# Writing out the hardware loops of the head stage and the expert stage

## The chip, the cores and the metric

The kernel runs on one core of a Trainium2 chip. The metric is the device time of one execution in microseconds (us), the median of three runs: 1520.96 us, from 1519.29 to 1521.52. The engines are PE (TensorE, matmuls; PEld is its weight load), DVE (VectorE), ACT (ScalarE), POOL (GpSimd) and SP (SyncE, which issues the DMAs). Each runs an instruction stream of its own; they meet in semaphores only.

## What is computed

One transformer block on x of 4 x 1024 x 128 in float32: a differential attention with 8 heads, then a feed-forward part in which each token's projections are weighted by 16 experts. Cut to what matters:

```python
x = x + attn(layernorm(x))          # B=4, T=1024, 8 heads, D=32, two sub-heads each
#   w = softmax(q1 k1) - lam * softmax(q2 k2);  y = w @ v;  y = gamma * y / rms(y);  y @ Wout
x = x + ffn(layernorm(x))
#   rw = gating(x)                                 # 16 experts
#   q, k, v = sum_e rw[e] * (x @ proj[e])          # head size 64
#   attn = softmax(causal(q k)) @ v                # within a batch
#   out = sum_e rw[e] * attn @ o_proj[e]
```

## The kernel before, in words

**Head stage.** A step is one pair of heads of one batch; there are 16 steps (`STEPS`) of 16 units (`UNITS`). A unit is 128 queries of one head, with its two sub-heads. The engines handle 32 units (`SLOTS`, two steps) in one piece of code, called a pass below, and there are eight passes (`ITERS`). Each engine has its own function for a pass: `slots(it, first, last)` on PE, ACT and DVE, `two_steps` on SP. Pass 0 is written out with `first` and pass 7 with `last`; passes 1 to 6 are one hardware loop, `Fori(1, ITERS - 1)`. POOL goes by half steps of 8 units: `units(h, tail)` stands in two loops, for h 0 to 1 and h 2 to 31.

For each unit PE makes the scores of a sub-head (`scores`, L584) in its half of `score_ps`, DVE takes the row maxima (L1207), ACT the exponentials with their sums (L900). DVE makes the factor of the second sub-head (L1218, L1220), POOL scales and adds (`mix`, L478 and L480), and three units later PE transposes the mixed rows (L607), ACT and DVE copy them to `probT` (L829, L322), and PE multiplies with v (L613). Beside it, at fixed places of a pass, `misc_fill` has PE make the projections of later steps (L562, L567), which ACT and DVE split into two float16 parts (L863, L1126) and SP restacks by DMA (L362). The rms of a finished half step is taken on POOL (`rms`, L485 to L491), and DVE scales by it (L1259).

**Expert stage.** A batch is eight token tiles; `tiles2(it, first, last)` on PE, ACT and DVE handles a batch. Batches 0 and 3 are written out, batches 1 and 2 are `Fori(1, B - 1)`. POOL scales tiles by the expert weights in pairs (L532) in `Fori(1, B * NT // 2)`; SP's part was written out already. DVE's L1412 runs once in each tile.

**What sets the order.** Each engine's order is that of its code; pools or a scheduler have no part in it. All buffers are reused under hand-written semaphore counts. In a loop such a count is an expression of the loop's variable, so it stands in a register and is computed before the wait:

```python
def mix(n, u):
    pool.wait_ge(c_ok, n + 1)
```

Here `n` is `8 * h + u`. Tile addresses that move with the loop go by registers too, such as `resid[:, bass.ds(tile0, 4), :]`.

Of the kernel before, what the change touches and what calls it, by code (L numbers as in the profile page):

```python
# [48 lines left out]
B, T, C = 4, 1024, 128  # L49
NT = T // P  # L50
# [3 lines left out]
STEPS = B * G  # L54
UNITS = 16
ITERS = STEPS // 2
# [86 lines left out]
def block_kernel(nc, x, wq, wkv, wout, lq1, lk1, lq2, lk2, gamma, sim, gates, eq, ek, ev, eo, out):  # L143
    ctx = ExitStack()
    with ctx:
# [183 lines left out]
        def _(sp):  # L329
# [53 lines left out]
            def two_steps(it, first, last):  # L383
                for k in range(2):
                    j = 2 * it + k

                    if not last:
                        token0, column0 = (j + 2) // G * T, (j + 2) % G * P
                        sp.wait_ge(filled["v1"], j + 1)
                        load_step(k, token0, column0)  # L390

                    if not (last and k == 1):
                        stack("k", (k + 1) % 2, j + 1, None if first and k == 0 else UNITS * j)

                    if not last:
                        stack("q", k, j + 2, UNITS * (j + 1))

            two_steps(0, True, False)
            sp.wait_ge(ln_late, 6)
            with sp.Fori(1, ITERS - 1) as it:  # L400
                two_steps(it, False, False)
            two_steps(ITERS - 1, False, True)

# [30 lines left out]
        def _(pool):  # L434
# [58 lines left out]
            def units(h, tail):  # L493

                for u in range(8):
                    mix(8 * h + u, u % 4)
                    if tail and u == RMS_AFTER:
                        rms(h - 2)

            with pool.Fori(0, 2) as h:  # L500
                units(h, False)
            with pool.Fori(2, 2 * STEPS) as h:
                units(h, True)

            pool.wait_ge(g_mean, 1)
# [22 lines left out]
            def scale_by_experts(m, r, peeled):  # L528

                if not peeled:  # L530
                    pool.wait_ge(xs_lo, m)
                pool.tensor_tensor(xs[:, r, :, :], x2n[:, bass.ds(m, 1), :].to_broadcast([P, E, C]),  # L532
                                   rw_all[:, bass.ds(m, 1), :].rearrange("p a e -> p e a").to_broadcast([P, E, C]),
                                   ALU.mult).then_inc(xs_ok, 1)

            scale_by_experts(0, 0, True)
            scale_by_experts(1, 1, False)
            with pool.Fori(1, B * NT // 2) as pair:
                scale_by_experts(2 * pair, 0, False)
                scale_by_experts(2 * pair + 1, 1, False)  # L540

# [2 lines left out]
        def _(pe):  # L544
# [124 lines left out]
                            mm.then_inc(out_ok, 1)  # L669

            slots(0, True, False)
            with pe.Fori(1, ITERS - 1) as it:
                slots(it, False, False)
            slots(ITERS - 1, False, True)

# [142 lines left out]
                    experts(3)  # L818

            tiles2(0, True, False)  # L820
            with pe.Fori(1, B - 1) as it:
                tiles2(it, False, False)
            tiles2(B - 1, False, True)

# [2 lines left out]
        def _(act):  # L827
# [111 lines left out]
                        rsqrt_seed(gs[:, 4, 0:BT], gs[:, 3, 0:BT], gs[:, 2, 0:BT], g_v, 1, g_y, 0)  # L939

            slots(0, True, False)
            with act.Fori(1, ITERS - 1) as it:
                slots(it, False, False)
            slots(ITERS - 1, False, True)

# [90 lines left out]
                                       ACT.Copy, scale=1.0 / WSCALE).then_inc(kv_read, 1)  # L1036

            tiles2(0, True, False)
            with act.Fori(1, B - 1) as it:
                tiles2(it, False, False)  # L1040
            tiles2(B - 1, False, True)

# [2 lines left out]
        def _(dve):  # L1045
# [217 lines left out]
                        ln2_early(s - LN2_SLOT)  # L1263

            slots(0, True, False)
            with dve.Fori(1, ITERS - 1) as it:
                slots(it, False, False)
            slots(ITERS - 1, False, True)

# [145 lines left out]
                                                 op0=ALU.mult, op1=ALU.subtract).then_inc(lo2, 1)  # L1415

            tiles2(0, True, False)
            with dve.Fori(1, B - 1) as it:
                tiles2(it, False, False)
            tiles2(B - 1, False, True)  # L1420

# [21 lines left out]
```

## Time and profile before

| | |
|---|---|
| median of three runs | 1520.96 us |
| profiled execution, its own time | 1519.09 us |
| its span, first to last instruction | 1517.3 us |
| granted TensorE clock, mean | 0.97 |
| instructions in the profile | 26450 |
| code brought by queue q8 | 36 packets, 0.59 MB |
| code brought by queue q14 | 49 packets, 0.40 MB |

The profile is of one execution. Busy time counts the instructions that do work; register, branch, wait and DMA-issuing instructions are not in it. An instruction that is queued begins a little before the one ahead of it ends, so back to back starts overlap by up to a tenth of a microsecond. "issue" as a releaser means that the engine waited for nothing that the profile shows. The granted clock is a share of 2.4 GHz. The head stage spans about 40 to 1130 us, the expert stage about 1190 us to the end; pass 1 begins at 170.

### The profile page before, as it was taken

To read this page: it belongs to the slowest core of one execution; us is meant where nothing else is said; L and a number is where in the kernel's file an instruction comes from. 1 tells how busy PE (TensorE), PEld (TensorE's weight loads), DVE (VectorE), ACT (ScalarE), POOL (GpSimd) and SP (SyncE) were. 2 spreads that over 40 slices of the span, in tenths; PEclk is the share of its full clock that TensorE was granted. 3 is DMA by queue.
4 is the path that set the end of the run, shared out by engine and by line. 5 is a ranking of instruction groups with operands and counts; after the bars stand their busy time and mean duration, and the time that the engine had idled before them with its cause. 6 is when DMAs were issued, how large, how long until landed. Compare 5 with 4: busy or idle time off the path is not lost. (4 is left out here: it accounts for less than half of the span.)

```text
span 1517.3 us, 26450 instructions
## 1 busy us (share of the span) xinstructions
PE 1259.6 (83%) x8370; PEld 745.9 (49%) x8370; DVE 1266.5 (83%) x2033; ACT 1038.6 (68%) x1871; POOL 1107.2 (73%) x715
## 2 busy tenths in 40 slices
PE   3788888888888888888888888888874179999997
PEld 1444444444444444444444444444433179889887
DVE  5898999989998999999999899999986557766664
ACT  2887777777777777777777777777754155555553
POOL 3898888888888888888888888888882443434320
PEclk9899999999999999999999999999996589999999
DMA  4231111111211111111211111111003377777670
GB/s 111 71 81 48 47 29 48 29 47 39 58 34 47 35 39 47 28 48 39 55 35 47 32 43 47 28 30 27 0 1 56 68 129 119 133 117 135 115 125 10
DMA packets 184565, 86.32 MB, mean 57 GB/s; under 512 B 150176, under 2 KB 166048, under 8 KB 184480
## 3 DMA queue, kind: packets, MB, share of 16 engines
q1 hardware_dynamic: 184480, 85.33, 26.4%
q8 instruction: 36, 0.59, 0.2%
q14 instruction: 49, 0.40, 0.1%
HBM read 7.68 MB, written 2.10 MB: 6 GB/s over the span
## 5 line engine op out<-in xcount | busy, mean ns | idle before, releaser
L1207 DVE TENSOR_REDUCE negmax<-score_ps 128x1 f32<-128x1024 f32 x512 | 618.7, 1216 | 87.1 <-PE score_ps L584 85.3
L900 ACT ACTIVATE prob<-score_ps,negmax 128x1024 f32<-128x1024 f32 x512 | 571.6, 1116 | 128.8 <-DVE negmax L1207 116.7
L480 POOL TENSOR_TENSOR prob<-prob 128x1024 f32<-128x1024 f32 x256 | 604.2, 2360 | 21.3
L584 PE MATMUL score_ps<-ka,qa 128*128 128x512 f16 x1024 | 312.4, 387 | 119.5 <-ACT prob L900 106.0
L478 POOL TENSOR_SCALAR prob<-prob,ccol 128x1024 f32<-128x1024 f32 x256 | 287.3, 1122 | 103.9 <-DVE ccol L1220 103.5
L607 PE MATMUL trans_ps<-ident,prob 128*128 128x128 f32 x2048 | 283.3, 276 | 7.4 <-POOL prob L480 3.0
L613 PE MATMUL attn_ps<-probT,v_sb 128*64 128x512 f32 x1024 | 276.6, 620 | 1.1 <-DVE probT L322 1.1
L607 PEld LDWEIGHTS trans_ps<-ident,prob 128*128 128x128 f32 x2048 | 239.5, 142 | 75.5 <-DVE probT L322 17.7
L532 POOL TENSOR_TENSOR xs<-xnT,rw_all 128x2048 f32 (+1 forms) x32 | 115.5, 3611 | 170.4 <-DVE prob L1352 163.7
L584 PEld LDWEIGHTS score_ps<-ka,qa 128*128 128x128 f16 x1024 | 72.4, 98 | 277.9 <-ACT prob L900 234.0
L322 DVE COPY probT<-trans_ps 128x512 f32<-128x512 f32 x256 | 173.9, 679 | 2.4 <-PE trans_ps L607 2.4
L736 PE MATMUL qkv_ps<-ew_split,xsT 128*128 128x192 f16 x1536 | 145.9, 250 | 31.5 <-DMA xsT<-prob 31.5
L829 ACT ACTIVATE probT<-trans_ps 128x512 f32<-128x512 f32 x256 | 152.4, 595 | 20.0 <-PE trans_ps L607 19.9
L736 PEld LDWEIGHTS qkv_ps<-ew_split,xsT 128*128 128x128 f16 x1536 | 129.9, 99 | 34.9 <-issue 31.6
L1352 DVE TENSOR_TENSOR prob<-xs,prob 128x2048 f16<-128x2048 f32 x32 | 73.4, 2292 | 65.8 <-ACT prob L973 65.8
L613 PEld LDWEIGHTS attn_ps<-probT,v_sb 128*64 128x64 f32 x1024 | 51.2, 135 | 109.4 <-issue 109.3
L900 ACT ACTIVATION_READ_ACCUMULATOR prob<-score_ps,negmax 128x1 f32 x512 | 103.1, 201 | 0.0
L973 ACT ACTIVATE prob<-xs 128x2048 f16<-128x2048 f32 x32 | 61.3, 1916 | 32.4 <-POOL xs L532 32.4
L1220 DVE TENSOR_SCALAR ccol<-recip,sums,lam 128x1 f32<-128x1 f32 x256 | 69.9, 273 | 9.4
L1259 DVE TENSOR_TENSOR attn_n<-attn_both,tl 128x512 f32<-128x512 f32 x32 | 72.2, 2257 | 0.1
L863 ACT ACTIVATE split<-misc_ps 128x512 f16<-128x512 f32 x60 | 35.8, 597 | 52.3 <-PE misc_ps L562 52.3
L1010 ACT ACTIVATE prob<-s_ps,nm 128x128 f32<-128x128 f32 (+7 forms) x32 | 23.7, 742 | 68.9 <-DVE nm L1387 68.9
(193 smaller groups left out, 1355.8 us busy)
## 6 DMA issues: line engine op xcount, KB each, us to landing
qa<-split SPq DMA_DIRECT2D x256, 64.0 KB, 2.0
ka<-split SPq DMA_DIRECT2D x256, 64.0 KB, 2.0
xg<-xnT SPq DMA_DIRECT2D x16, 512.0 KB, 3.0
resid<-in_L_attn_x SPq DMA_DIRECT2D x4, 512.0 KB, 5.6
wg<-in_L_attn_Wkv SPq DMA_DIRECT2D x32, 64.0 KB, 1.9
out<-yo SPq DMA_DIRECT2D x32, 64.0 KB, 2.5
wg<-in_L_attn_Wq SPq DMA_DIRECT2D x16, 64.0 KB, 1.9
xsT<-prob SPq DMA_TRANSPOSE x64, 4.5
```

Of the source, the lines that this page charges most:

```text
L322: copy(probT[:, half % 2, 4 * bank:4 * bank + 4, u // 4, (u % 4) * P:(u % 4 + 1) * P], trans_ps[:, bank, :].rearrange("p (k q) -> p k q", ...
L478: pool.tensor_scalar(prob2[:, u, :], prob2[:, u, :], ccol[:, u:u + 1], 1.0, ALU.mult, ALU.mult).then_inc(scaled_P, 1)
L480: pool.tensor_tensor(prob1[:, u, :], prob1[:, u, :], prob2[:, u, :], ALU.add).then_inc(mix_ok, 1)
L532: pool.tensor_tensor(xs[:, r, :, :], x2n[:, bass.ds(m, 1), :].to_broadcast([P, E, C]), rw_all[:, bass.ds(m, 1), :].rearrange("p a e -> p e ...
L584: mm = pe.matmul(score_ps[:, sub, kh * HALF:(kh + 1) * HALF], qa[:, par, head * 2 + sub, q0:q0 + P], ka[:, par, head * 2 + sub, kh * HALF: ...
L607: mm = pe.transpose(trans_ps[:, kb, t * P:(t + 1) * P], prob1[:, u % 4, k0:k0 + P], ident[:, :])
L613: return pe.matmul(attn_ps[head * DV:(head + 1) * DV, :], v_sb[:, (half // 2) % 2, kt, head * DV:(head + 1) * DV], probT[:, half % 2, kt, ...
L736: mm = pe.matmul(qkv_ps[:, 0:3 * DE], xsT[:, t % X_BUFS, x_part, e, :], ew_split[:, w_part, e, :], start=e == 0 and n == 0, stop=e == E - ...
L829: return act.activation(dst, src, ACT.Copy)
L900: act.activation(prob2[:, s % 4, :] if sub else prob1[:, s % 4, :], score_ps[:, sub, :], ACT.Exp, bias=negmax[:, s % 2, sub:sub + 1], accu ...
L1207: dve.tensor_reduce(negmax[:, s % 2, sub:sub + 1], score_ps[:, sub, :], AX.X, ALU.max, negate=True).then_inc(max_ok, 1)
L1352: dve.tensor_tensor(xs_split[:, r, 1, :, :], xs[:, r, :, :], xs_split[:, r, 0, :, :], ALU.subtract).then_inc(xs_lo, 1)
```

## The change

All hardware loops of the two stages are written out: the loop's body is emitted once for each value, `it`, `h` and `pair` are Python integers, and so every count that is waited for and every address is a constant. Nothing else is changed: the same work in the same order on each engine. The nine places:

```diff
@@ sync: two_steps
-            with sp.Fori(1, ITERS - 1) as it:
+            for it in range(1, ITERS - 1):
                 two_steps(it, False, False)
@@ gpsimd: units
-            with pool.Fori(0, 2) as h:
+            for h in range(2):
                 units(h, False)
-            with pool.Fori(2, 2 * STEPS) as h:
+            for h in range(2, 2 * STEPS):
                 units(h, True)
@@ gpsimd: expert stage
-            with pool.Fori(1, B * NT // 2) as pair:
+            for pair in range(1, B * NT // 2):
                 scale_by_experts(2 * pair, 0, False)
                 scale_by_experts(2 * pair + 1, 1, False)
@@ tensor, scalar and vector, head stage (pe, act, dve)
-            with pe.Fori(1, ITERS - 1) as it:
+            for it in range(1, ITERS - 1):
                 slots(it, False, False)
@@ tensor, scalar and vector, expert stage (pe, act, dve)
-            with pe.Fori(1, B - 1) as it:
+            for it in range(1, B - 1):
                 tiles2(it, False, False)
```

In the order of the program ACT has 744 rows before (waits shown) and 1319 with the change, POOL 112 and 673 rows. The end of ACT's head loop, before (L900 the exponential, L829 the copy to `probT`, L863 the split of a projection, L942 the loop itself):

```order
L895 ISA
L900 ACTIVATE prob,sums<-score_ps,negmax 128x1024 [waits trans_ok,max_ok]
L829 ACTIVATE probT<-trans_ps 128x4x128 [waits trans_ok]
L895 REGISTER_ALU
L900 ACTIVATE prob,sums<-score_ps,negmax 128x1024 [waits mix_ok,max_ok]
L863 ACTIVATE split<-misc_ps 128x512 [waits filled_q1]
L942 REGISTER_ALU
L942 COMPARE_AND_BRANCH
```

The same place of ACT with the change, between pass 1 and pass 2:

```order
L900 ACTIVATE prob,sums<-score_ps,negmax 128x1024 [waits trans_ok,max_ok]
L829 ACTIVATE probT<-trans_ps 128x4x128 [waits trans_ok]
L900 ACTIVATE prob,sums<-score_ps,negmax 128x1024 [waits mix_ok,max_ok]
L863 ACTIVATE split<-misc_ps 128x512 [waits filled_q1]
L900 ACTIVATE prob,sums<-score_ps,negmax 128x1024 [waits trans_ok,max_ok]
L829 ACTIVATE probT<-trans_ps 128x4x128 [waits trans_ok]
L900 ACTIVATE prob,sums<-score_ps,negmax 128x1024 [waits mix_ok,max_ok]
L933 ACTIVATE attn_nT<-misc_ps 128x512 [waits cols_ok]
```

The register arithmetic and the jump are gone; L863 is followed by the exponential of the next pass.

POOL inside `units`, before (L478 and L480 are `mix`, L485 to L491 `rms`; L476 is the wait of `mix`, L484 to L490 those of `rms`):

```order
L476 REGISTER_ALU
L478 TENSOR_SCALAR prob<-prob,ccol 128x1024 [waits c_ok]
L480 TENSOR_TENSOR prob<-prob 128x1024 [waits scaled_P]
L484 ISA
L485 TENSOR_TENSOR tl<-tl 128x8 [waits stat_ok]
L486 ISA
L487 TENSOR_TENSOR tl<-tl 128x8 [waits rms_v]
L488 REGISTER_ALU
L489 TENSOR_TENSOR tl<-tl,rms_const 128x8 [waits rms_v]
L490 REGISTER_ALU
L491 TENSOR_TENSOR tl<-tl,rms_const 128x8 [waits rms_v]
L476 REGISTER_ALU
```

And with the change:

```order
L478 TENSOR_SCALAR prob<-prob,ccol 128x1024 [waits c_ok]
L480 TENSOR_TENSOR prob<-prob 128x1024 [waits scaled_P]
L485 TENSOR_TENSOR tl<-tl 128x8 [waits stat_ok]
L487 TENSOR_TENSOR tl<-tl 128x8 [waits rms_v]
L489 TENSOR_TENSOR tl<-tl,rms_const 128x8 [waits rms_v]
L491 TENSOR_TENSOR tl<-tl,rms_const 128x8 [waits rms_v]
L478 TENSOR_SCALAR prob<-prob,ccol 128x1024 [waits c_ok]
```

The instructions that do the work stand as before, and what computed the counts between them is gone.

## Rows read from the trace of the kernel before

**Rows 1.** The page, busy us (share of the span) xinstructions of each engine

```profile
PE 1259.6 (83%) x8370; PEld 745.9 (49%) x8370; DVE 1266.5 (83%) x2033; ACT 1038.6 (68%) x1871; POOL 1107.2 (73%) x715
```

**Rows 2.** Windows of L478: stretch, us, POOL busy (x starts), PEclk, DMA share, GB/s

```profile
136.39:170.35 33.96, 8.98 (x8) 1.00 0.14 32
170.35:272.24 101.89, 26.94 (x24) 1.00 0.18 46
272.24:342.45 70.21, 17.95 (x16) 0.98 0.16 41
342.45:410.37 67.92, 17.95 (x16) 1.00 0.16 42
410.37:479.02 68.65, 17.95 (x16) 1.00 0.16 42
...
546.94:615.60 68.66, 17.96 (x16) 1.00 0.16 42
...
683.51:752.45 68.94, 17.96 (x16) 1.00 0.16 41
...
820.37:889.25 68.88, 17.95 (x16) 1.00 0.16 41
889.25:1025.09 135.84, 35.88 (x32) 1.00 0.15 37
```

**Rows 3.** Waits, 170.35 to 1025.09 us: engine, line, releaser: us, times, longest

```profile
ACT prob L900 <- DVE negmax L1207: 83.4, 145, 2.0
POOL prob L478 <- DVE ccol L1220: 82.1, 105, 1.8
PE score_ps L584 <- ACT prob L900: 79.7, 130, 2.9
DVE negmax L1207 <- PE score_ps L584: 63.9, 127, 1.3
...
ACT prob L900 <- issue: 10.9, 5, 2.4
```

**Rows 4.** Timeline of ACT, second jump: start, us, instruction, [idle before]

```profile
437.43 0.60 ACT L863 ACTIVATE split<-misc_ps 128x512 f16<-128x512 f32 x1 [0.59 <-PE misc_ps L562]
440.10 1.11 ACT L900 ACTIVATE prob<-score_ps,negmax 128x1024 f32<-128x1024 f32 x1 [2.07 <-issue]
```

**Rows 5.** Timeline of DVE at the same jump

```profile
437.50 2.40 DVE L1259 TENSOR_TENSOR attn_n<-attn_both,tl 128x512 f32<-128x512 f32 x1
439.83 0.15 DVE L1218 RECIPROCAL recip<-sums 128x1 f32<-128x1 f32 x1
```

**Rows 6.** DMA queues (packets, MB, share), 170 to 305.8 us, then 305.8 to 442

```profile
q8 instruction: 5, 0.08, 0.3%
q14 instruction: 8, 0.07, 0.2%
...
q14 instruction: 5, 0.04, 0.1%
```

**Rows 7.** Windows, all engines: PE, PEld, DVE, ACT, POOL busy, PEclk, DMA share, GB/s

```profile
300.00:302.00 2.00, 0.57 (x6) 0.33 (x3) 1.96 (x3) 0.00 (x0) 1.22 (x1) 1.00 0.01 4
...
304.00:306.00 2.00, 2.00 (x6) 0.39 (x6) 1.90 (x4) 0.82 (x2) 1.91 (x1) 0.50 0.26 59
```

**Rows 8.** Timeline of POOL, in the loop, then in the tail behind it

```profile
189.76 0.21 POOL L485 TENSOR_TENSOR tl<-tl 128x8 f32<-128x8 f32 x1
190.04 0.21 POOL L487 TENSOR_TENSOR tl<-tl 128x8 f32<-128x8 f32 x1
...
1133.55 0.20 POOL L485 TENSOR_TENSOR tl<-tl 128x8 f32<-128x8 f32 x1
1133.83 0.20 POOL L487 TENSOR_TENSOR tl<-tl 128x8 f32<-128x8 f32 x1
```

**Rows 9.** Windows of L1412 on DVE, expert stage

```profile
1249.32:1322.25 72.93, 2.24 (x8) 1.00 0.71 123
1322.25:1395.24 72.99, 2.24 (x8) 1.00 0.71 124
1395.24:1468.06 72.82, 2.24 (x8) 1.00 0.70 121
```

More of the change, by code:

```diff
@@ L941, in _ @@
             slots(0, True, False)
-            with act.Fori(1, ITERS - 1) as it:
+            for it in range(1, ITERS - 1):
                 slots(it, False, False)
@@ L1038, in _ @@
             tiles2(0, True, False)
-            with act.Fori(1, B - 1) as it:
+            for it in range(1, B - 1):
                 tiles2(it, False, False)
@@ L1265, in _ @@
             slots(0, True, False)
-            with dve.Fori(1, ITERS - 1) as it:
+            for it in range(1, ITERS - 1):
                 slots(it, False, False)
@@ L1417, in _ @@
             tiles2(0, True, False)
-            with dve.Fori(1, B - 1) as it:
+            for it in range(1, B - 1):
                 tiles2(it, False, False)
```

## The prediction

> **What bounds the kernel now.** The busy shares come first [rows 1]: PE and DVE at 83% each, POOL 73%, ACT 68%. No engine is full, so the stages are read apart. The loops of the change lie in two of them. The head stage runs eight passes of 32 units (pass 0 and pass 7 were written out already, passes 1 to 6 are the loop); the expert stage runs four batches of eight token tiles (the loop holds batches 1 and 2).
>
> A unit of the head stage has exactly one L478 on POOL, so a stretch between two L478 starts measures the pace of the whole pipeline, whatever sets it [rows 2]. Eight written-out units of pass 0 take 33.96 us. Twenty-four units inside pass 1 take 101.89, which is 33.96 for eight. Sixteen units inside a later pass take 67.92, again 33.96 for eight (three more such stretches, left out there, read the same to 0.01). In the waits of this part [rows 3] PE waits for ACT's exponentials (79.7 us), ACT for DVE's row maxima (83.4), DVE for PE's scores (63.9), POOL for DVE's factors (82.1). That is a ring of three engines around the score buffer, with POOL beside it.
>
> The stretches that hold the jump back from one pass to the next are longer [rows 2]. ACT's waits name a cause [rows 3]: five times it waited for nothing that the profile shows, 10.9 us together, always in front of L900, the exponential; it has no other such wait in the whole span. Around the second jump [rows 4] ACT ends L863 at 438.03 us and begins L900 at 440.10, 2.07 us later. What may happen in those two microseconds shows in the queues that bring code [rows 6]. In the stretch of pass 1, q8 brings five packets and q14 eight. In the next pass q8 brings none and q14 still five. Packets keep coming though each pass runs the same code, so the loop of some engine does not fit the memory it is run from. I take it to be ACT's, because ACT alone stands still at the jump.
>
> **The change part by part.**
>
> 1. ACT's jump in the head stage, five times (between passes 1 and 2, and so on to 5 and 6; at the end of pass 6 the loop is left and ACT falls through). The order shows the jump between L863 and L900 gone and nothing in its place. Its price is not the 10.9 us, since ACT has idle time anyway; it is what the stretches of [rows 2] are longer by than 67.92:
> 70.21 - 67.92 = 2.29; 68.65 - 67.92 = 0.73; 68.66 - 67.92 = 0.74; 68.94 - 67.92 = 1.02; 68.88 - 67.92 = 0.96. The sum is **5.74 us**. The last 32 units, to 1025.09, are 135.84, four times 33.96: where the loop is left, nothing is lost.
> Why is the first jump the dearest? PE was busy for only 0.57 of the 2 us from 300 to 302, and just behind, from 304 to 306, the granted clock was 0.50, the lower of its two levels (1.2 instead of 2.4 GHz), while PE was busy throughout [rows 7]. In the stretches of the four other jumps the mean is 1.00 [rows 2]. So some 1.4 us of the 2.29 (2.29 less 0.73 to 1.02) is the clock, and I let it go with the stall. The lower bound of this part is five of the small ones, 5 x 0.73 = 3.7 us; the upper bound is all of ACT's idle time, 10.9 us. I take 5.74, measured end to end on another engine.
>
> 2. The jumps of the other engines. DVE issues its jump right behind L1259. This takes 2.40 us, and L1218, the first instruction of the next pass, begins at 439.83 without idle time before it [rows 5]. So the jump costs 0, covered by L1259, as long as it needs less than that; without the cover I would price it like ACT's, 2.07 us of idleness. POOL jumps thirty times in the head stage, each time beside L480, which is already running: 0, and behind that cover lie its 82.1 us of waiting [rows 3]. PE brings no code after pass 1 [rows 6] and its jump lies in its waits for ACT: 0.
> The Trainium skill ("Runtime: NRT & Kernel Launch", section "Instruction fetch mechanics") says that most engines hold two pages of 16 KiB of code, and that a taken branch to a page outside them forces a fetch before execution goes on. By that rule DVE, whose loop has more rows in the order than ACT's, reloads at its jumps too, and the sum would be up to 5 x 2.07 = 10 us larger, an estimate, if nothing covered it. The trace agrees for ACT's standstill; of DVE it shows no idle time, and its packets on q14 are of half that size (0.04 MB in five).
>
> 3. Register arithmetic and waits on registers, gone from all engines (the order shows it on ACT and POOL). ACT, DVE, PE and SP had constants in pass 0 and registers in pass 1, and both have 33.96 us [rows 2]. POOL was in a loop in both, so it needs its own rows: L485 and L487 stand 0.07 to 0.08 us apart both in the loop (189.76 + 0.21, then 190.04) and in the tail on constants (1133.55 + 0.20, then 1133.83) [rows 8]. Cost 0. If instead each of POOL's eleven such gaps in eight units shrank by 0.04 us, POOL would need 0.4 us less for eight units and only wait longer for L1220 in its 82.1 us.
>
> 4. The expert stage. DVE's L1412 runs once for each tile [rows 9]. Eight tiles take 72.93 us where the first four are written out, 72.99 where all are in the loop, 72.82 where the last four are written out. The difference of 0.06 to 0.17 for four tiles makes 0.1 to 0.3 for a batch. The loop has two batches: I take **0.2 us** and keep 0 to 0.7.
>
> 5. What is added is code. Written out, PE's five further passes bring their five packets each again, and DVE, POOL and SP bring theirs. Pass 1 did just this on PE, DVE and ACT at once and kept 33.96 us for eight units. Cost 0, covered by the run time of the code already there (five packets of PE in 136 us, 27 us each). Without the cover a packet costs what [rows 4] show, 2.07 us of idleness. SP issues the same DMAs in the same order, their addresses now constants, and none of the waits of [rows 3] is for one.
>
> Sum: 5.74 + 0.2 = 5.9 us. The profiled execution took 1519.09 us (its span is 1517.3, the rest lies around it), so it would have been 1513.2. It lies 1.87 below the median of the three runs, 1520.96, against which I forecast **1515.0 us**.
>
> **The rivals.**
> A. *The stall only moves.* For it: ACT is idle a third of the time [rows 1], and the ring has waits at every place. Against it: the stretches of [rows 2] are longer by 0.7 to 2.3 us, and no later one is shorter. It gives 1520 to 1521.
> B. *Streaming starves an engine* (slower). Straight code has to be fetched in time. Five passes bring five packets of PE more and, by my estimate from [rows 6] (eight less the five of ACT), three of other engines: 40 pieces. If each held its engine up as ACT's reload does at its cheapest, 40 x 0.73 = 29 us come against 5.7 gone: 1544 us. It decides from 5.74 / 40 = 0.14 us a piece. Against it are pass 1 and the expert stage's first batches. For it is only that no trace here shows so long a stretch of straight code.
> C. *More than the stalls goes*: the ring gains from constants at places that passes 0 and 1 hide, or the stalls' recovery reaches further than my stretches. Half of the way to the upper bound of part 1 is 2.6 us more: 1512.
> D. *The change doesn't do what it says*: ACT's straight code stops at the borders of its pieces as it does at the jump. That ACT has such a wait nowhere but at the five jumps [rows 3], though passes 0 and 7 are straight code, speaks against it. It gives 1519 to 1521.
>
> **How the numbers follow.** The forecast has a chance of 0.72, C 0.08, A and D together 0.13, B 0.07. The three runs differ by about 0.15% (1519.29 to 1521.52), and I call no change what is within 0.2%, or 3.0 us: 1517.9 and less is faster. The forecast and C are faster (0.80), A and D the same (0.13), B slower (0.07). The forecast's own bounds, 3.7 to 5.7 + 0.7 = 6.4 us off, give 1514.5 to 1517.3, and a median's noise of 1.1 us on either side makes it 1513.4 to 1518.4. The lower end 1511.5 takes in C, the upper end 1519.5 a part of A and D. B and the rest of A and D are left out.
>
> **What would show it.** Right: no wait of ACT at L900 without a releaser; every sixteen units between 272 and 889 us in 67.9; a clock without the dip at 304; q8 up from 36 packets to some 65, q14 from 49 to some 55 to 65; eight tiles at 72.9. Wrong: idle time without a releaser at regular distances on PE, DVE or ACT (B, D); a head stage of the old length with more waiting of PE for ACT (A); less than 33.9 us for eight units (C).

## The result and the profile after

The changed kernel took **1511.3 us** (median of four runs, 1509.07 to 1513.36) against 1520.12 (four runs, 1518.12 to 1521.52): a ratio of 0.9943 [0.9924, 0.9961], 8.8 us or 0.57% faster. The forecast was 1515.0 with a range from 1511.5 to 1519.5: the direction is right, the gain is half as large again as the 5.9 us forecast, and the median lies 0.2 us below the range.

One figure is easily misread. The profiled execution after took 1513.36 us (span 1511.5) where my sum gave 1513.2 for it. But it was the slowest of its four, and the profiled one of before (1519.09) one of the faster of its own. The two profiles differ by 5.7 us, the medians by 8.8: the profiled execution of after lies 2.1 us above its median, that of before 1.0 below. Both numbers need an explanation.

From the page: busy time and instructions of each engine, then the queues that bring code (packets, MB, share). They answer to [rows 1]; before, the whole span had 36 and 49 packets.

```profile
PE 1264.6 (84%) x8370; PEld 750.2 (50%) x8370; DVE 1265.5 (84%) x2033; ACT 1037.3 (69%) x1871; POOL 1106.5 (73%) x715
...
q8 instruction: 68, 1.11, 0.3%
q14 instruction: 52, 0.43, 0.1%
```

The work is the same, instruction for instruction; more code is brought.

Windows of L478 on POOL, one start for each unit (stretch, us, POOL busy (x starts), PEclk, DMA share, GB/s), at the places of [rows 2]:

```profile
136.53:170.45 33.92, 8.97 (x8) 1.00 0.14 32
170.45:272.22 101.77, 26.95 (x24) 1.00 0.18 46
272.22:340.07 67.85, 17.97 (x16) 1.00 0.17 42
340.07:407.94 67.87, 17.97 (x16) 1.00 0.17 43
407.94:475.77 67.83, 17.96 (x16) 1.00 0.16 42
475.77:543.88 68.11, 17.96 (x16) 1.00 0.17 43
543.88:611.74 67.86, 17.95 (x16) 1.00 0.16 42
...
679.58:747.42 67.84, 17.96 (x16) 1.00 0.17 42
...
815.28:883.14 67.86, 17.94 (x16) 1.00 0.17 43
```

The five stretches with a jump, which had 70.21, 68.65, 68.66, 68.94 and 68.88 us, now have 67.83 to 67.87. One stretch has 68.11, 0.25 more than its neighbours; it returns below.

Waits, 170.45 to 1018.84 us, the answer to [rows 3] (us, times, longest):

```profile
ACT prob L900 <- DVE negmax L1207: 92.9, 150, 2.1
POOL prob L478 <- DVE ccol L1220: 76.3, 100, 1.3
PE score_ps L584 <- ACT prob L900: 66.2, 125, 1.0
DVE negmax L1207 <- PE score_ps L584: 56.4, 100, 1.1
POOL prob L478 <- issue: 0.2, 1, 0.2
```

ACT's wait on nothing is gone, and PE's longest wait for ACT fell from 2.9 us to 1.0. ACT's timeline at the place of [rows 4] shows the two instructions back to back; L900 has no idle time before it:

```profile
434.98 0.60 ACT L863 ACTIVATE split<-misc_ps 128x512 f16<-128x512 f32 x1 [0.66 <-PE misc_ps L562]
435.48 1.11 ACT L900 ACTIVATE prob<-score_ps,negmax 128x1024 f32<-128x1024 f32 x1
```

Windows of L1412, the expert stage's tiles by eights, the answer to [rows 9]:

```profile
1244.42:1317.05 72.63, 2.25 (x8) 1.00 0.74 129
1317.05:1389.62 72.57, 2.24 (x8) 1.00 0.74 124
1389.62:1462.20 72.58, 2.24 (x8) 1.00 0.71 126
```

Set end to end, the two profiled executions differ by 5.73 us, and these are its pieces:

| stretch (counted in L478, later L1412) | before | after | difference |
|---|---|---|---|
| from the end of [rows 2]'s second stretch, 176 units (five jumps) | 752.85 | 746.62 | -6.23 |
| next 16 units | 68.74 | 68.68 | -0.06 |
| to the fourth expert tile | 155.48 | 156.90 | +1.42 |
| next 24 expert tiles | 218.74 | 217.78 | -0.96 |
| all the rest | | | +0.10 |

The row with +1.42 holds one more fall of the clock. Windows of all engines (PE, PEld, DVE, ACT, POOL busy, PEclk, DMA share, GB/s), first of before, then of after:

```profile
1054.00:1062.00 8.00, 5.80 (x25) 2.74 (x21) 6.74 (x11) 4.63 (x9) 6.70 (x5) 0.79 0.01 2
1084.00:1092.00 8.00, 4.93 (x24) 1.88 (x24) 7.96 (x9) 3.64 (x6) 6.70 (x5) 1.00 0.00 0
```

```profile
1084.00:1092.00 8.00, 5.96 (x28) 3.58 (x27) 6.38 (x10) 5.53 (x10) 6.92 (x4) 0.79 0.01 2
```

These windows lie in the last pass of the head stage, which PE, ACT and DVE had written out before as well. There the granted clock fell once in the profiled execution of before (at 1058 us) and twice in that of after (at 1052 and 1086 us; 0.79 over 8 us is some 3.4 us at the lower level). What a fall costs shows in the row of 16 units above it: over all fourteen profiled executions they take 68.57 to 68.80 us with a fall and 67.33 to 67.44 without, 1.3 us. The second fall is no property of the change: e4 below, the same program as after, has no fall near 1090 and takes 154.79 us in the row of 156.90.

### The profile page after: what moved, and what is told of

Its sections match the earlier page's. It is cut to its first block and busy times, and to the rows that moved or that the text cites. A ratio compares the mean times of both kernels' runs of the same rounds, so it can differ in the third digit from the quotient of the medians.

```text
span 1511.5 us, 24183 instructions
## 1 busy us (share of the span) xinstructions
PE 1264.6 (84%) x8370; PEld 750.2 (50%) x8370; DVE 1265.5 (84%) x2033; ACT 1037.3 (69%) x1871; POOL 1106.5 (73%) x715
## 5 line engine op out<-in xcount | busy, mean ns | idle before, releaser
L900 ACT ACTIVATE prob<-score_ps,negmax 128x1024 f32<-128x1024 f32 x512 | 571.5, 1116 | 127.3 <-DVE negmax L1207 126.2
L480 POOL TENSOR_TENSOR prob<-prob 128x1024 f32<-128x1024 f32 x256 | 604.3, 2360 | 21.3
L478 POOL TENSOR_SCALAR prob<-prob,ccol 128x1024 f32<-128x1024 f32 x256 | 287.3, 1122 | 99.2 <-DVE ccol L1220 98.8
L532 POOL TENSOR_TENSOR xs<-xnT,rw_all 128x2048 f32<-128x2048 f32 x32 | 115.6, 3611 | 169.4 <-DVE prob L1352 162.6
L829 ACT ACTIVATE probT<-trans_ps 128x512 f32<-128x512 f32 x256 | 152.5, 596 | 20.8 <-PE trans_ps L607 20.8
L900 ACT ACTIVATION_READ_ACCUMULATOR prob<-score_ps,negmax 128x1 f32 x512 | 102.8, 201 | 0.0
L1259 DVE TENSOR_TENSOR attn_n<-attn_both,tl 128x512 f32<-128x512 f32 x32 | 72.3, 2260 | 0.1
L863 ACT ACTIVATE split<-misc_ps 128x512 f16<-128x512 f32 x60 | 35.8, 597 | 52.7 <-PE misc_ps L562 52.7
```

Of the source, the lines that this page charges most:

```text
L478: pool.tensor_scalar(prob2[:, u, :], prob2[:, u, :], ccol[:, u:u + 1], 1.0, ALU.mult, ALU.mult).then_inc(scaled_P, 1)
L480: pool.tensor_tensor(prob1[:, u, :], prob1[:, u, :], prob2[:, u, :], ALU.add).then_inc(mix_ok, 1)
L829: return act.activation(dst, src, ACT.Copy)
L900: act.activation(prob2[:, s % 4, :] if sub else prob1[:, s % 4, :], score_ps[:, sub, :], ACT.Exp, bias=negmax[:, s % 2, sub:sub + 1], accu ...
```

## The experiments

Two theories stood at the start. The first (J in the expectations): all of the gain is ACT's five standstills, and they come from where ACT's loop lies in its pieces of code. The rival (R): the gain is spread over engines, or comes of constants in place of registers. Later a third question was added: why the median gained more than the profile's sum.

**Which engine.** First ACT's loop of the head stage alone, then all loops but that one.

```
 # e1_act_head_only: the kernel before with
-            with act.Fori(1, ITERS - 1) as it:      (slots, line 942)
+            for it in range(1, ITERS - 1):
 # e2_all_but_act_head: the other nine lines of the change (ten in all, not nine), not this one
```

> Only ACT's loop of the head stage is written out, all others stay loops. If the gain is the end of ACT's standstill at the five jumps (theory J), this alone gives nearly all of it: some 1513 us against 1520, no wait of L900 without a releaser, sixteen units in 67.9 us throughout. If constants in place of registers give it (theory R), spread over all engines, this gives about a fifth: 1518 to 1519, and the gain of each eight units would be the same in all passes.

> The change without its part on ACT's head loop, which stays a loop. Theory J: the five standstills of 2.1 us stay, and so do the longer stretches (68.6 to 70.2 us for sixteen units); only what the rest gives is left, 0.03 us for eight units and up to 1 us in the expert stage: 1518 to 1519. Theory R: most of the gain stays, 1512 to 1513.

Measured, against 1523.10 us of the kernel before on that chip (17 runs): e1 1511.96, ratio 0.9935 [0.9922, 0.9949]; e2 1521.12, ratio 0.999 [0.9981, 0.9999]. In e1 the five stretches with a jump have 67.92 to 67.95 us and ACT has no wait on nothing. In e2 nine loops are written out and the stall is as it was. Waits of e2 over the head stage:

```profile
ACT prob L900 <- issue: 11.1, 5, 2.3
```

and its windows of L478 around the five jumps:

```profile
270.80:341.33 70.53, 17.95 (x16) 0.98 0.16 41
409.17:478.14 68.97, 17.95 (x16) 1.00 0.16 42
546.23:616.16 69.93, 17.97 (x16) 0.98 0.16 41
684.00:754.44 70.44, 17.94 (x16) 0.98 0.16 41
822.29:891.06 68.77, 17.96 (x16) 1.00 0.17 42
```

By the medians one line of the ten carries 11.1 of the 12.7 us that the whole change brings on this chip (below); each has an interval of some 2 us on either side. And one thing is new: at three of the five jumps the clock fell (0.98 over the stretch), and those stretches are 1.0 to 1.8 us longer than the two others. In [rows 2] only the first jump showed that.

**Why ACT.** If ACT's loop is a little too long for the memory it is run from only because it begins late in a piece of code, then moving the whole loop, without unrolling anything, must cure it; and moving it by a whole piece must not. A piece is 8 KB by the queue's row (five packets, 0.04 MB [rows 6]); at 64 bytes, my assumption, it holds 128 instructions. So 60 dummy instructions are put ahead of everything on ACT, and in the control 128. All loops stay.

```
 # e3_act_padded_60 (f3_act_padded_128: 128 in place of 60)
             act.preload_act_table_set(...)
+            for _ in range(60):
+                act.sem_inc(padding, 1)
```

> The kernel before with all its loops, and 60 semaphore increments that nobody waits for at the start of ACT's stream, where it waits for inputs. They shift ACT's head loop (342 instructions) from a place where it touches four pieces of code of 128 instructions to one where it touches three. Theory J with its cause (the loop and the piece fetched ahead don't fit together): no standstill at the jumps, q14 down by some 25 packets, 1513 to 1514 us, as if written out. If the jump itself costs the 2 us, whatever the place of the code: 1520 as before.

> As the run with 60 semaphore increments at the start of ACT's stream, but with 128 of them, a whole piece of code, so that the loop begins at the same place within its piece as in the kernel before. If the place of the loop within the pieces decides: five standstills of about 2.1 us and the code packets of q14 as before or one more. If the increments themselves help: no standstill.

Measured: e3 1513.99, ratio 0.9943 [0.993, 0.9957], with every loop of the kernel before still there. Its stretches with the first, second and fifth jump (its lines are shifted, POOL's is L479), then those of f3 with the first and second:

```profile
271.75:339.66 67.91, 17.95 (x16) 1.00 0.16 42
407.58:475.49 67.91, 17.94 (x16) 1.00 0.16 42
...
815.07:882.99 67.92, 17.94 (x16) 1.00 0.16 42
```

```profile
276.23:346.53 70.30, 17.95 (x16) 0.98 0.16 41
414.43:483.07 68.64, 17.94 (x16) 1.00 0.16 42
```

ACT's timeline of e3 at the second jump, with the jump executed and nothing idle before the exponential:

```profile
434.63 0.60 ACT L866 ACTIVATE split<-misc_ps 128x512 f16<-128x512 f32 x1 [0.58 <-PE misc_ps L563]
435.13 1.11 ACT L903 ACTIVATE prob<-score_ps,negmax 128x1024 f32<-128x1024 f32 x1
```

The queues agree. In e3, q14 brings no packet at all between 306 and 577 us, through two jumps; in f3 it brings five in the pass behind the first jump (309 to 447 us), as before [rows 6], and four in the next (447 to 580 us). The page of e3 has

```profile
q14 instruction: 25, 0.20, 0.0%
```

against 49 before. The waits of f3 have the standstill back, at L903 as that line is called there:

```profile
ACT prob L903 <- issue: 10.5, 5, 2.3
```

The jump itself shows too. In ACT's stream the next instruction comes 0.24 to 0.27 us behind it in e3, and 2.4 to 2.7 us behind it before. So a jump costs nothing when the loop fits, and the fit depends on where the loop begins. f3 as a whole took 1522.62 us, one execution; its 128 instructions run ahead of the first unit, which begins some 4.5 us later, so that time says nothing, but its stretches do.

**Does DVE's cover hold.** The prediction held that DVE's jump costs nothing because L1259 covers it. 50 dummy instructions on DVE make its loop reload too.

```
 # f4_dve_padded_50
+            for _ in range(50):
+                dve.sem_inc(padding, 1)
             dve.wait_ge(const2_in, 16 * 2)
```

> Fifty semaphore increments at the start of DVE's stream push its head loop (301 instructions) from three pieces of code to four. If the memory holds four pieces and one of them is always fetched ahead, DVE now fetches at its jumps too: q14 up by 20 to 30 packets. My part 2 said that L1259 covers it: then no idle time of DVE without a releaser and the same stretches as before. If the cover is too short, DVE stands still for up to 2 us and each stretch with a jump grows by up to 1 us more.

The page has `q14 instruction: 75, 0.61, 0.1%` in place of 49: 26 packets more, about five for each jump. DVE's timeline at the second jump, where L1262 is what L1259 was:

```profile
437.28 2.40 DVE L1262 TENSOR_TENSOR attn_n<-attn_both,tl 128x512 f32<-128x512 f32 x1
439.61 0.15 DVE L1221 RECIPROCAL recip<-sums 128x1 f32<-128x1 f32 x1
```

No idle time between them, no wait of DVE on nothing in the whole head stage, and jump stretches of 70.32 and four times 68.64 us, as before. So the reload is covered, but not by L1259 (L1262 here) alone. The jump and the next instruction of DVE's stream at this place, by line L1269 (its times are to 0.1 us):

```profile
L1269 DVEq COMPARE_BRANCH  x1: 63/63/63, 435.7 to 435.7; - x1
L1269 DVEq FUSED_REGOPS  x1: 62/62/62, 438.5 to 438.5; - x1
```

Over the five jumps 2.76 to 2.85 us lie between the two, against 0.33 to 0.37 before. That is more than the 2.40 us of L1262. What saves DVE is that its stream runs ahead of its work: at 435.75 us, when the jump is executed, L1210 is running and L323 and L1262 are still to come, so that DVE has work until 439.68, 3.9 us. ACT at its jump has only the last 0.5 us of L863.

**The other loops one by one.**

```
 # f1_pool_head_only:      lines 500 and 502 (POOL, head stage)
 # f2_expert_only:         lines 538, 821, 1039, 1418
 # g2_experts_pool_only:   line 538
 # g3_experts_pe_only:     line 821
 # g4_all_but_pool_head:   the whole change but lines 500 and 502
```

> Only POOL's two loops of the head stage are written out. With the change eight units take 33.92 us instead of 33.96, also where ACT alone stays a loop; where ACT alone is written out they take 33.96. If POOL's register arithmetic is it: 33.92 here. If it is that of DVE, PE or SP: 33.96. ACT's five standstills stay in either case, and a good part of them is followed by a drop of the clock, as in the run with all but ACT written out.

> Only the loops of the expert stage are written out. Eight tiles take 72.6 us here instead of 72.8 to 73.0 if constants give it; 72.9 if what changed them was the state in which the head stage leaves the machine. The head stage stays as it was, with its standstills.

> Only POOL's loop over pairs of tiles in the expert stage is written out. Eight tiles 72.6 us if POOL's registers were the 0.2 to 0.4 us of a batch; 72.8 to 73.0 if those of PE, ACT or DVE were.

> Only PE's loop over batches in the expert stage is written out. PE is the busiest engine there, so if one engine's waits on registers are in the way it is PE's: 72.6 us for eight tiles. If it is ACT or DVE: 72.8 to 73.0.

> The change, but POOL's head loops stay. They never stood still at a jump, and written out they show one wait of 0.2 us and a longer stretch (34.18 instead of 33.93 us) at the unit where a new piece of POOL's code begins. Head stage like the change (no standstill), eight units 33.93 to 33.96, without the one 34.18. Time 1510 to 1511, the same as the change within its interval, or up to 1 us less if the clock does not fall at 1052 us, where it fell with the change but not with ACT alone written out.

f1 took 1521.25 and f2 1521.93 where the kernel before, measured beside them, took 1520.88 (one execution each, so no difference can be read). Both keep the standstills. f1 has 33.93 us for eight units, and the odd 0.25 us of after at the same units (480.02 to 548.13, 68.11 us) with the same wait of POOL on nothing, 0.2 us once. In g4, where POOL's head loops stay, that stretch is 67.86. So the 0.25 is a price of the written-out POOL code.

For the expert stage the tiles of f2, with all of its loops written out, and of g2 and g3, with POOL's and PE's alone (windows of L1412, columns as above):

```profile
1253.14:1325.79 72.65, 2.24 (x8) 1.00 0.72 124
1325.79:1398.36 72.57, 2.24 (x8) 1.00 0.72 126
1398.36:1470.93 72.57, 2.24 (x8) 1.00 0.72 123
```

```profile
1248.90:1321.70 72.80, 2.24 (x8) 1.00 0.72 124
1321.70:1394.44 72.74, 2.24 (x8) 1.00 0.71 125
1394.44:1466.94 72.50, 2.24 (x8) 1.00 0.70 121
```

```profile
1247.69:1320.48 72.79, 2.24 (x8) 1.00 0.72 122
1320.48:1393.35 72.87, 2.23 (x8) 1.00 0.73 127
1393.35:1466.15 72.80, 2.24 (x8) 1.00 0.71 124
```

Against 218.74 us before [rows 9] that is -0.95 for f2, -0.70 for g2 (218.04) and -0.28 for g3 (218.46). Of the expert stage's gain POOL's loop has some three quarters and PE's the rest; by subtraction nothing is left for ACT and DVE, whose loops were not tried alone. Each is one execution, but these stretches hardly differ between executions: 218.69 to 218.78 us in the seven that keep all loops of the stage (before, e1, e3, f1, f3, f4, g1), and -0.93 to -1.01 in the five that have none (after, e2, e4, f2, g4). So neither g2 nor g3 came out as expected, 72.6 or 72.8 to 73.0 throughout: the gain is shared. Why POOL's loop costs anything, though POOL waits 132.1 us for DVE in these stretches of before, isn't shown.

g4 took 1510.42 (median of five), ratio 0.9949 [0.9936, 0.9963] against 1519.22 on its chip (nine runs): the change without POOL's head stage is as good as the change, and no version here is clearly better than either.

**The size.** The change once more, on the chip of e1 to e3, and the kernel before once more.

```
 # e4_change_again: the change
 # g1_before_again: the kernel before
```

> The change once more, beside the others on one chip. If the 8.8 us between the first medians are real: ratio 0.994 and a profiled time near 1511. If the profiled 5.7 us are the size and the rest was the spread of four runs: ratio 0.996.

> The kernel before, one more profiled execution. So far 30 jumps of ACT with a standstill: 11 with a drop of the clock behind them cost 1.8 to 2.7 us each (mean 2.3), 19 without one 0.7 to 1.1 (mean 0.8). If that is the whole of it, the five stretches here fall into the same two groups by whether the clock falls, and nothing else in 170 to 1025 us differs from the first profile.

e4 took 1510.42, ratio 0.9923 [0.991, 0.9936]: 12.7 us between the medians, 9.7 to 13.7 by the interval. The first measurement gave 8.8 us, 5.9 to 11.6 by its interval. A gain of 5.9 us is a ratio of 0.9961: the second interval leaves it out, the first just reaches it. g1 (1520.03) is the same program as before, and in it the clock fell at two jumps. Two of its windows of L478 with a jump, and one without:

```profile
271.83:342.10 70.27, 17.91 (x16) 0.98 0.16 41
342.10:409.95 67.85, 17.86 (x16) 1.00 0.16 42
...
820.09:889.86 69.77, 17.87 (x16) 0.98 0.16 41
```

The fifth jump has 69.77 us here and 68.88 in [rows 2]: nothing but the execution differs. And g1 runs at 33.93 us for eight units against 33.96 before, which misses my expectation that nothing else would differ. It also takes from the change what I had begun to give it: the 0.03 us for eight units between [rows 2] and after lie between executions and are no effect of constants.

Put all jumps together, of the nine profiled executions in which ACT stands still (before, e2, f1 to f4, g1 to g3), each stretch less its own execution's pace:

| | jumps | mean longer by | from, to |
|---|---|---|---|
| clock did not fall | 28 | 0.82 us | 0.70 to 1.12 |
| clock fell within the stretch | 17 | 2.24 us | 1.72 to 2.67 |

At the first jump it fell in all nine; at the others in 8 of 36. In the five profiled executions without standstills (after, e1, e3, e4, g4) it fell nowhere between 60 and 1040 us.

## Why the prediction was wrong in size and right in kind

**Part 1, ACT's jumps: the mechanism holds, the term was mis-sized.** e1 and e2 show that the gain is ACT's, e3 and f3 that it is the loop's place in the code. The step that failed is its price: "In the stretches of the four other jumps the mean is 1.00", and with it "I take 5.74, measured end to end on another engine". I read off one execution what a jump costs and took its clock as given. That execution was one in which only one jump in five was answered with a fall. A fall costs 2.24 - 0.82 = 1.42 us, and nine executions of kernels with the standstill had one, two or three of them at jumps, 1.9 on average. With these the term is 5 x 0.82 + 1.9 x 1.42 = 6.8 us, where I had 5.74. The same comes out directly: the 176 units take 753.6 us on average in the nine and 746.8 in the five without standstills.

That the profiled execution was a mild one could have been seen. It took 1519.09, 1.87 us below the median. I wrote that distance down and carried it over unchanged, as if it lay outside the standstills. On the chip of e1 to e4, the runs of the kernel before have a mean clock of 0.964 to 0.966 and 1520.5 to 1524.2 us, but for one with 0.970 and 1518.82; the profiled run of before, with 1519.09, is of that one's kind. The five runs of e4 have 0.971 or 0.972. One fall, 3.4 us at the lower level, lowers the mean by about 0.001.

What the medians add to this. With n falls at jumps the gain is 5 x 0.82 + 1.42 n + 0.94 for the experts, an estimate: 6.5 us for n = 1, 7.7 for 1.9, 9.3 for n = 3. Measured were 8.8, whose interval holds all three, and 12.7, whose interval leaves even n = 3 just out, so up to 3.4 us of the 12.7 stay open. One part that the formula lacks is in the traces: behind the loops, in the row of 155.48 us, the nine executions with standstills take 155.5 to 157.5 us (mean 156.6) and the five without 154.4 to 156.9 (mean 155.4). That is 1.2 us more, in a stretch where no jump of ACT stalls, and no run shows whether it belongs to the change or to the executions; after and e4, one program, differ there by 2.1. The mean clocks (0.965 against 0.972) suggest that the open part is the clock's too, but they also count the time between the stages, where executions of one program differ: from 1110 to 1240 us the clock is 0.75 in before and 0.72 in g1. And on the chip of g1 to g4 the kernel before had one run at 0.972 with 1517.27 us, while g4 at 0.972 takes 1510.42 and 1510.08: 7 us at equal mean clock, where five stalls without a fall and the experts make 5.0.

Of the profiled pair, where n = 1, the term held: 5.74 forecast, and 6.23 measured over the 176 units. In these lie 22 x 0.03 = 0.66 of the pace that differs between executions, and against it 0.25 of POOL's new cost; 5.82 are the jumps. That the two whole profiles differ by 5.73 us, beside the 5.9 of my sum, is luck: the 176 units gave 0.5 and the experts 0.8 more than forecast, and the row with the fall of the clock behind the loops took 1.4 back.

Of the 3.7 us by which the forecast missed, 0.8 lie in its start: I set out from 1520.96, and the kernel before measured 1520.12 beside the change.

**Part 2, the other engines' jumps at 0: right, with the cover misread.** f4 gave DVE's jump a reload, and nothing moved. But "covered by L1259, as long as it needs less than that" fails: the jump with its reload took 2.8 us, L1259 takes 2.40, and the cover was the 3.9 us of work that DVE still had when it jumped. Before, DVE's jump took 0.33 to 0.37 us and needed no cover. I also wrote that DVE's loop is longer than ACT's; in instructions it is shorter, 301 against 342. The Trainium skill's rule ("Runtime: NRT & Kernel Launch", section "Instruction fetch mechanics"), two pages of 16 KiB for most engines, would have DVE reload at its jumps as ACT does. No run here bears that out for ACT and DVE: packets of 8 KB, ACT's loop cured by 60 instructions and not by 128, and no reload on DVE until it too is shifted. What would fit all of these is four pieces of 8 KB, in total as much as those two pages. ACT's loop has 342 instructions: it would touch four pieces where it lies, and with one fetched ahead need a fifth; shifted by 60 it would touch three. That reading is mine, not shown by a row. The same section's other rule, that a taken branch to a place outside forces a fetch, the traces agree with: 2.04 to 2.36 us of idle time at each such jump of ACT.

**Part 3, constants in the head stage at 0: right.** e2 has them on all engines but ACT and keeps the old time to within 0.1%, of which the experts are half.

**Part 4, the expert stage: mis-sized, 0.2 forecast, 0.94 measured**, just above the 0.7 that I kept as its upper end. The 0.2 was already the low end of my own working, 0.1 to 0.3 for each of two batches. I compared the loop's tiles with those written out next to them, 72.99 against 72.82 and 72.93. But the first and the last stretch hold four tiles of each kind, and POOL's loop ran through all three. The comparison was blind to three quarters of the effect. Of the signs that I had named, "eight tiles at 72.9" is the one that failed: they take 72.6.

**Part 5, the added code at 0: right but for 0.25 us**, POOL's one wait on nothing. q8 came to 68 packets where I said some 65; q14 to 52, a little under my 55 to 65. That q8 serves PE, which I took for granted, shows in g3: with PE's expert loop alone written out q8 brings 43 packets in place of 36, and q14 49 as before.

**The rivals.** A (the stall only moves) is refuted by the stretches: none with a jump is longer than its neighbours. B (streaming starves an engine) is refuted: 32 more packets on q8, and 0.25 us in all. D is refuted by e1. C (more goes than the stalls) has the right size, 1512 against 1511.3. Its second half, that the recovery reaches further, comes nearest: but the fall of the clock behind a jump lies inside my stretches, and it was its frequency that I had wrong. Whether anything reaches beyond them is the open part above.

## What to carry to other kernels

When an engine stands idle with no releaser at a loop's jump, and its code queue keeps bringing packets through a loop that never changes, the loop lies badly in its pieces of code: write it out, or shift it with dummy instructions (60 cured it here, 128 did not). The shift alone gave 0.9943. A reload is covered only by the work that the engine still has before it when it jumps: 0.5 us on ACT, 3.9 on DVE, for a reload of 2.4 to 2.9. Price a stall over several executions: set the profiled run's time and mean clock beside those of the timed runs, and if it is among the fastest, the stall may cost more than its trace shows. To judge a loop by its neighbours, make sure that the neighbours are not in a loop on another engine.

## What the runs showed of the hardware that was not expected

The clock's answer to a standstill is not decided by the length of PE's idle time alone. Timeline of PE in e2, the first two jumps:

```profile
302.07 1.03 PE L584 MATMUL score_ps<-ka,qa 128*128 128x512 f16 x2 [2.86 <-ACT prob L900]
```

```profile
440.41 0.60 PE L584 MATMUL score_ps<-ka,qa 128*128 128x512 f16 x2 [2.84 <-ACT prob L900]
```

The idle time is the same, 2.86 and 2.84 us. Behind the first the granted clock went to 0.50, the lower level (1.2 instead of 2.4 GHz), and the two matmuls took 1.03 us; behind the second it stayed at 1.00, and they took 0.60. What decides between the two is open. It was not tried, since no edit at hand changes it alone. Equally open is why the clock falls near 1050 and 1090 us in some executions and not in others, with standstills or without. These falls are part of why runs of one kernel scatter by some 3 us.

And a dummy instruction is not free where nothing covers it: with 128 increments at the start ACT is idle for 7.7 us before its first activation (f3), at most 0.06 us for each, and the first unit begins 4.5 us later. The 60 of e3 left the first unit where it was, at 41.9 us.
